# Six landings in the first batch's instructions, gone through by TensorE in four visits at the start of a layer kernel

## What is computed

```python
x = x + attention(layernorm(x), Wq, bq, Wk, bk, Wv, bv, Wo, bo)
#   q, k = elu(proj) + 1;  per chunk:
#   num = tril(q k^T) v + q S;   den = q . (cumsum(k) + z)
#   out = num / den;  S = S + k^T v;  z = z + sum(k)
x = x + 0.5 * (silu(hf @ w1 + fc1_bias) @ w2 + fc2_bias)
#   hf = layernorm(x) * gamma + beta
#   w1, w2 = (q - 128) * scales, groups of 128 rows
```

## Time and profile before

| what | value |
|---|---|
| median of 3 runs | 1390.42 us (1386.1 to 1390.5) |
| the profiled execution, its own time | 1389.24 us |
| span of that execution, first to last instruction | 1387.5 us |
| TensorE busy | 1362.3 us, 25658 matmuls |
| VectorE, ScalarE, GpSimd busy | 1189.3, 1070.0, 672.8 us |
| mean granted clock of TensorE | 0.996 |

### The profile page before, as it was taken

The page is one execution under the profiler, slowest core; times in us unless marked ns, Lnnn a source line. Parts: engine busy times, 40 slices in busy tenths (PEclk is TensorE's granted clock), DMA queues, the critical chain, the costliest instruction groups (busy, mean ns, idle before and its releaser), DMA issues.

```text
span 1387.5 us, 60917 instructions
## 1 busy us (share of the span) xinstructions
PE 1362.3 (98%) x25658; PEld 1226.9 (88%) x25658; DVE 1189.3 (86%) x1952; ACT 1070.0 (77%) x1750; POOL 672.8 (48%) x512
## 2 busy tenths in 40 slices
PE   7889999999999999999999999999999999999998
PEld 6788899988899988999988999888999888999887
DVE  8878988888888889888889888889888888888876
ACT  4678777878778887778887778887788787788863
POOL 4644444554443545444545444544445554445454
PEclk9999999999999999999999999999999999999999
DMA  6111211211211221211222212212112212112110
GB/s 186 42 44 45 60 45 47 58 46 45 60 41 50 53 53 45 60 37 54 45 47 58 55 39 57 45 45 60 44 48 53 52 45 60 40 51 51 40 31 31
DMA packets 93525, 71.89 MB, mean 52 GB/s; under 512 B 8768, under 2 KB 92992, under 8 KB 93504
## 3 DMA queue, kind: packets, MB, share of 16 engines
q1 hardware_dynamic: 92144, 71.59, 20.7%
q10 hardware_dynamic: 1360, 0.01, 0.1%
HBM read 38.03 MB, written 16.78 MB: 39 GB/s over the span
## 4 chain that ended last, share of the span: by engine, by line
PE 94%; DVE 2%; issue 1%; DMA 1%; POOL 1%; SPq 0%; ACT 0%; POOLq 0%; DVEq 0%
PE sc L315 25%; PE ring L315 19%; PE num L485 7%; PE num L315 7%; PE sc L455 5%; PE sc L376 5%; PE sc L377 5%; PE num L499 4%; PE ring L376 3%; PE ring L377 3%; PE ring L468 2%; PE num L358 2%; PE ring L441 2%; PE sc L349 1%; PE num L376 1%
## 5 line engine op out<-in xcount | busy, mean ns | idle before, releaser
L1159 POOL TENSOR_TENSOR s_lo<-silu_f,s_hi 128x512 fp32r<-128x512 f32 x252 | 325.1, 1294 | 453.1 <-ACT s_hi L970 452.9
L963 ACT ACTIVATE silu_f<-silu_f 128x512 f32<-128x512 f32 x252 | 157.8, 626 | 28.8 <-DVE silu_f L700 27.7
L708 DVE TENSOR_TENSOR probs<-sc,causal 128x1024 f32<-128x1024 f32 x128 | 150.7, 1219 | 16.1 <-PE sc L455 13.6
L970 ACT ACTIVATE s_hi<-silu_f 128x512 fp32r<-128x512 f32 x252 | 153.7, 621 | 1.3
L315 PE MATMUL sc<-w_hi,s_hi 128*128 128x256 f32 x488 | 137.2, 281 | 0.0
L315 PE MATMUL sc<-w_lo,s_hi 128*128 128x256 f32 x488 | 137.1, 281 | 0.0
L315 PE MATMUL sc<-w_hi,s_lo 128*128 128x256 f32 x488 | 137.1, 281 | 0.0
L956 ACT ACTIVATE silu_f<-ring,bias,scale 128x512 f32<-128x512 f32 x93 | 72.4, 779 | 83.0 <-PE ring L377 80.1
L1195 POOL TENSOR_TENSOR ln_rstd<-ln_in,minus_half 128x8 f32<-128x8 f32 x32 | 52.6, 1643 | 169.8 <-DVE ln_in L801 169.8
L315 PE MATMUL ring<-w_hi,s_lo 128*128 128x256 f32 x480 | 134.9, 281 | 0.0
L315 PE MATMUL ring<-w_lo,s_hi 128*128 128x256 f32 x480 | 134.9, 281 | 0.0
(11 more groups left out here) (206 smaller groups left out, 4329.7 us busy)
## 6 DMA issues: line engine op xcount, KB each, us to landing
x_in<-in_x SPq DMA_DIRECT2D x32, 512.0 KB, 4.8
xb<-in_x SPq DMA_DIRECT2D x32, 512.0 KB, 3.5
rb<-den_rows SPq DMA_DIRECT2D x256, 64.0 KB
out<-out_t SPq DMA_DIRECT2D x64, 256.0 KB, 2.2
probs<-in_q SPq DMA_DIRECT2D x2, 512.0 KB, 8.1
silu_f<-in_q SPq DMA_DIRECT2D x2, 512.0 KB, 7.1
res<-in_sc SPq DMA_DIRECT2D x1, 512.0 KB, 7.1
out_t<-in_sc SPq DMA_DIRECT2D x1, 512.0 KB, 9.6
```

The costliest lines, as they stand in the source:

```text
L708: masked.done(e.tensor_tensor(probs[:, t, 2 * h:2 * h + 2, :, :, :].rearrange("p g m a q -> p (g m a) q"), sc[:, 2 * h:2 * h + 2, :].rearr ...
L963: silu.done(e.activation(slot(j, A), slot(j, A), ACT.Silu))
L970: sh.done(e.activation(s_hi[:, j, :], slot(j, A), ACT.Copy))
L1159: sl.done(e.tensor_tensor(s_lo[:, j, :], slot(j, A), s_hi[:, j, :].bitcast(F32), ALU.subtract))
```

## The change

Two helpers are added to TensorE's stream. landing_here puts a few instructions in the place where it is called: a branch over the landing, and the landing itself, a nop and a branch to wherever way_out says. In the ordinary run through batch 0 the landing is jumped over. visit branches to the first of its landings, each landing goes on to the next one of the visit, and the last one goes back behind the visit. So TensorE's sequencer executes one nop in each of the places and returns; no data is touched. There are four calls of visit in the prologue, with one, two, two and one landing, and six landings in batch 0: behind scores(0), chunk_states, values(0), values(1), from_states(0) and project_kq(3).

```diff
--- before.py
+++ after.py
@@ -323,13 +323,36 @@
                     ((lhs[0][:, t, toks], lhs[1][:, t, toks]), (w_hi[n][:, t, :], w_lo[n][:, t, :])) for t in range(T)])
             event.done(last)
 
+
+
+
+        outside, way_out = {}, {}
+
+        def visit(e, *landings):
+            back = f"{landings[0]}_back"
+            for landing, following in zip(landings, landings[1:] + (back,)):
+                way_out[landing] = following
+            e.br(landings[0])
+            parent = nc.switch_bb(back).parent
+            for landing in landings:
+                outside[landing] = parent
+
+        def landing_here(e, landing):
+            e.br(f"{landing}_over")
+            with nc.body(landing, parent=outside[landing], valid_engines=[e.engine]):
+                e.nop()
+                e.br(way_out[landing])
+            nc.switch_bb(f"{landing}_over")
+
         def pe_iteration(e, i, A, Fn, N, N2, preparation=None):
             w = Waiter(e, i)
             present = {u for u in USES if (Fn if u in FFN_USES else N if u in NEXT_USES else A)}
 
             def first_transposes():
+                visit(e, "first_scores_landing")
                 for n in range(WARM):
                     e.matmul(bank(SPARE[0])[:, 0:P], ident[:, :], ident[:, :], start=True, stop=True)
+                visit(e, "second_scores_landing", "first_values_landing")
                 for c in range(C):
                     if c < C - 1:
                         e.wait_ge(p_xhat, c + 1)
@@ -545,23 +568,30 @@
                 preparation["kq"]()
                 for n in range(2 * T):
                     project_kq(n)
+                visit(e, "second_values_landing", "states_landing")
                 preparation["v"]()
                 preparation["values"]()
                 project_v(0)
                 project_v(1)
+                visit(e, "projections_landing")
                 return
             if not Fn:
                 k_transposes(0)
                 k_transposes(1)
                 scores(0)
+                landing_here(e, "first_scores_landing")
                 denominators()
                 chunk_states()
+                landing_here(e, "second_scores_landing")
                 scores(1)
                 values(0)
+                landing_here(e, "first_values_landing")
                 values(1)
+                landing_here(e, "second_values_landing")
                 x_transposes(0)
                 x_transposes(1)
                 from_states(0)
+                landing_here(e, "states_landing")
                 from_states(1)
                 project_kq(0)
                 project_kq(1)
@@ -570,6 +600,7 @@
                 output_projection(0)
                 output_projection(1)
                 project_kq(3)
+                landing_here(e, "projections_landing")
                 project_v(0)
                 project_v(1)
                 w.need(phi, 1, 0)
```

## The result

| | kernel before | changed |
|---|---|---|
| median | 1391.38 us (21 runs) | 1394.63 us (21 runs, 1392.25 to 1403.02) |
| ratio | 1 | 1.0029, 95% interval 1.0019 to 1.0038 |
| profiled execution | 1389.24 us, span 1387.5 | 1403.02 us, span 1401.3 |

The change makes the kernel 0.29% slower by the ratio, some 4 us; the two medians themselves lie 3.25 us (0.23%) apart. The profiled execution is the longest of the 21; a second profile further down gave a span of 1394.8 with the same visits, and where the two differ it is said.

A forecast was written before the change was run, and what follows sets the result against it. TensorE, busy 98% of the span, was taken as the bound. Visits making the start 3.2 us late, less 1.3 us arriving from removed stalls, plus 0.1 for branches: 2.0 us slower, median 1392.4 us, range 1388.0 to 1399.5.

The forecast's parts named there:

- Stalls as fetches, blocks of 256 instructions, blocks 1 to 6 for the landings: TensorE's batch 0 stalls are fetches of 256-instruction blocks; landings lie in blocks 1 to 6; removing both stalls frees 3.6 us.
- Fetches in line, each asked for on entering the one before: Prologue visits: entering a block asks for the next, so five fetches (blocks 2 to 6) queue; k_transposes 3.2 us late.
- rival (c): A visit asks for its own block only; start 8.6 to 10.6 us late, median 1397.8 to 1401.5; chance 0.18.
- F of 4.4 and 3.9 us: Length of an unhidden block fetch in the visits: 4.4 us under DMA load, 3.9 after; 5.7 throughout gives 7.7 us late.
- The prediction's own sign of a wrong sum: The sum would be wrong if a fetch during the load of the weights takes over 6 us.
- The three stalls of the loop's first pass stay: Loop's first pass: stalls of 1.38, 1.11 and 2.66 us remain, as no landing lies in blocks from 7 on.
- The cap by rb: output_projection(0) waits for gt_lo, which needs the broadcast reciprocals at 38.5; of 3.6 to 5.0 us only 1.3 arrives.
- The clock of 1.0 in 30 to 40: Sign: granted clock 1.0 in 30 to 40 us, where it was 0.87 and 0.79 in the ten us from 30.
- Rival (b): Prologue visits are covered by TensorE's wait for x_hat; 1.3 to 2.4 us gained, median 1388.0 to 1389.1; chance 0.22.
- Rival (d): Visited blocks are gone before batch 0 needs them, so stalls remain; +3.3 us, 1393.7 (1392.2 to 1398.2); chance 0.10.

The follow-up runs named there:

- no_first_visit: The changed kernel without the visit of block 1 and without its landing; one execution, 1398.28 us.

## Why the prediction was right, and where not

The forecast was 1392.4 us and the measured median 1394.63; as ratios, 1.0014 forecast (2.0 of 1390.42) and 1.0029 measured. The sign and the mechanism (visits wait in line for fetches, and what they remove is capped) hold. That the number came so near is luck: the start was three times as late as forecast, and a term put at nothing, the loop's first pass, gave most of the excess back. Step by step:

- **Stalls as fetches, blocks of 256 instructions, blocks 1 to 6 for the landings**: right. Both stalls of batch 0 are gone in all versions that visit blocks 2 and 3 in order.
- **Fetches in line, each asked for on entering the one before**: right (no_first_visit), so rival (c) falls. My sign for (c), no packet before 5 us, was wrong: the packet was inside 7.0 to 8.2 though block 2 had been asked for at 3.0. The lateness at k_transposes, 9.6 to 10.0 us, lies where (c) had put it (8.6 to 10.6), but by longer fetches, not by missing requests.
- **F of 4.4 and 3.9 us**: the term that was mis-sized. It measured 6.5, 5.0, 7.1, 3.2 and 6.2 us. The step that failed is "nearer the low end, as the 16 KB packet itself took 1.2 us in light and in loaded stretches alike": the packet is as short as I said, but under load it begins 2.6 to 4.7 us after the request instead of 0.7 to 1.0. And the load was not over for block 6, as forecast: from its request at 24.9 to its packet at 28.8 the DMA share was 0.54; with the loads of w2 moved away it was 0.00 behind that request, and the packet began 0.8 us after it. The prediction's own sign of a wrong sum, a fetch of over 6 us during the load, came true. scores(0) was forecast 3.2 us late and came 9.6 to 10.0 late; even the end with F = 5.7 gave only 7.7. The signs named for it missed as far: the first packet at 7.1 instead of 3.7, the transposes at 14.85 instead of 11.4.
- **"The three stalls of the loop's first pass stay"**: wrong, and this hid the error of F. Together they had 5.2 us (5.8 in the second profile of before); in the changed kernel one of them is gone and the others have 3.1 us, 2.1 in its second profile. Together with the clock this gave back about 5 us between the second profiles. I had looked for landings in these blocks, and not asked what the shift of their borders does.
- **The cap by rb**: right as a mechanism. L764 waited 3.27 us for rb and TensorE 2.75 us for gt_lo; the reciprocals' delay passes to rb (issues at 38.35 instead of 27.18). The size fits too: where nothing was late at the start (three visits of present blocks), the product with rb started at 38.41 and output_projection(0) at 42.11, forecast were 38.5 and 42.1 (in the other profile of that version, 42.87).
- **The clock of 1.0 in 30 to 40**: not so. The low stretch moved to where TensorE now stands still, 10 to 20 us, with 0.66 against 1.00 before, and another piece lies at 32 us (0.83 in 30 to 40, as before).
- **Rival (b)**, covered visits: not for this change. But three visits at the right moments are covered, and then the gain is larger than its 1.3 to 2.4 us, since the first pass adds to it.
- **Rival (d)**, blocks that don't stay: not for blocks visited in order (14 packets), true for a block visited out of order (16 packets, stall back). The Trainium skill, "Runtime: NRT & Kernel Launch", section "Instruction fetch mechanics", says that prefetch is purely sequential and that the instruction memory holds only two lines. With the first half the trace agrees: each block asked for its successor alone, and one entered by a jump over others was fetched again later. The second half does not agree, as six blocks were kept here; the same section's own figure for TensorE's instruction memory, 128 KiB or 2048 instructions, is eight such blocks and does agree, which the prediction left out.

## What to carry to other kernels

Code that is fetched while it is needed shows up as "issue" in a table of waits; counting instructions between two such stalls tells the block size, and a short detour into a block brings the next one in early. Make the detour only into a block that is already there: it then costs half a microsecond and asks for its successor, while a detour into a missing one held the whole engine for 1.5 to 7.9 us here, the longer the more the DMA engines had to do and the later the block had been asked for. And where instructions are added ahead of a large loop, look at the first pass of the loop as well: the borders of its blocks move with them.

## What the runs showed of the hardware that was not expected

- A 16 KB instruction packet takes 0.9 to 1.5 us in any load (once 1.9). In the visits it began 1.2 to 5.5 us after the request while the DMA engines moved 165 to 391 GB/s, and 0.7 to 1.0 us after it at 99 GB/s or less.
- Blocks fetched by branches in ascending order without a gap are kept; after a jump over blocks 2 and 3 two blocks were fetched again.
- A branch to a landing that is there takes 0.32 to 0.43 us, one from a landing on or back 0.18 to 0.19 us. The Trainium skill, "Advanced Engine Details and Errata", section "Control Flow Timing", gives 51 ns for an unconditional branch and 108 ns for a compare-and-branch; no branch of these visits was as short; the branch of the loop's own condition (L621) took 75 ns in most passes.
- From the entry of block 9 to the packet of block 10 it took 3.1 to 3.8 us or 1.2 to 1.5 us, with the border four products apart. What in between holds the request back is not known.
